# Routing in three groups of tiles and an expert-by-expert result combine, in a Perceiver block with a mixture of experts

## The reference, cut to what matters

```python
xf = layernorm(x).reshape(T, 512)
logits = xf @ gate_w.T                          # 8 experts
probs = softmax(logits)
top_p, top_i = top_k(probs, 2)
w = top_p / (sum(top_p) + 1e-9)
capacity = int(1.25 * T / 8)                    # 160
oh = one_hot(top_i, 8)
rank = cumsum(oh, axis=0) - 1                   # per choice k and expert, over the tokens
keep = sum(rank * oh) < capacity
comb = einsum(w * keep, oh)                     # (T, 8)
for e in range(8):
    y = (silu(xf @ gate_proj_w[e].T) * (xf @ up_proj_w[e].T)) @ down_proj_w[e].T
    out = out + comb[:, e:e+1] * y              # hidden width 1024
x = x + out
```

## Time and profile before

| | us |
|---|---|
| median of 3 runs (range) | 1016.68 (1015.19 to 1021.68) |
| profiled execution, device time | 1016.95 |
| its span in the trace | 1015.2 |
| TensorE busy in the span | 996.6 |
| VectorE busy | 618.2 |
| ScalarE busy | 397.7 |
| GpSimd busy | 210.7 |

### The profile page before, as it was taken

One profiled execution on the slowest core, in us unless ns is written; L12 is line 12 of the kernel. 1 busy time (PEld: TensorE's weight loads), 2 busy tenths in 40 slices (PEclk: granted clock), 3 DMA queues, 4 the chain that ended last, 5 costly groups with the idle time before them and its releaser, 6 DMA issues.

```text
span 1015.2 us, 14027 instructions
## 1 busy us (share of the span) xinstructions
PE 996.6 (98%) x5188; PEld 761.7 (75%) x5188; DVE 618.2 (61%) x1191; ACT 397.7 (39%) x638; POOL 210.7 (21%) x188
## 2 busy tenths in 40 slices
PE   7999999999999999999999999999999999999998
PEld 4886444444454558878888888898999999999997
DVE  6268443445656565896466766677666666656666
ACT  2332211213111143355667542534544544445441
POOL 2053400002000036454422124720000000000051
PEclk9999999999999999999999998999999999999999
DMA  9809589999999922023311100885664656645443
GB/s 290 316 1 389 242 341 422 406 410 396 411 390 408 375 81 82 1 86 112 109 46 34 32 2 6 303 264 174 183 196 139 204 168 184 186 154 181 153 143 135
DMA packets 45511, 206.91 MB, mean 204 GB/s; under 512 B 5536, under 2 KB 16032, under 8 KB 41232
## 3 DMA queue, kind: packets, MB, share of 16 engines
q1 hardware_dynamic: 40256, 187.95, 51.4%
q0 software_dynamic: 5200, 18.22, 5.1%
HBM read 190.04 MB, written 16.12 MB: 203 GB/s over the span
## 4 chain that ended last, share of the span: by engine, by line
PE 87%; DVE 8%; issue 1%; ACT 1%; DMA 1%; SPq 0%; POOL 0%; ACTq 0%; DVEq 0%
PE ps L476 28%; PE ps L892 20%; PE ps L908 10%; PE ps L640 9%; PE ps L611 8%; PE ps L470 1%; PE ps L588 1%; PE ps L621 1%; DVE stats L1278 1%; PE ps L644 1%; PE ps L933 1%; ACT w L1203 1%; PE ps L802 1%; DMA xr<-in_x 1%; PE ps L522 1%
## 5 line engine op out<-in xcount | busy, mean ns | idle before, releaser
L892 PE MATMUL ps<-x,w 128*128 128x320 f32 x1536 | 235.3, 309 | 2.2 <-DVE x L1861 1.1
L892 PEld LDWEIGHTS ps<-x,w 128*128 128x128 f32 x1536 | 230.0, 188 | 7.6 <-DVE w L1802 1.4
L1802 DVE TENSOR_TENSOR w<-big,w 128x1536 fp32r<-128x1536 f32 x64 | 112.4, 1758 | 80.7 <-ACT w L1203 80.1
L908 PE MATMUL ps<-w,hsplit 128*128 128x512 f32 x512 | 128.8, 393 | 0.0
L1203 ACT CAST w<-big 128x1536 fp32r<-128x1536 f32 x64 | 94.4, 1479 | 29.5 <-PE ps L908 29.5
L908 PEld LDWEIGHTS ps<-w,hsplit 128*128 128x128 f32 x512 | 93.3, 188 | 16.5
L611 PE MATMUL ps<-big 128*64 128x512 f32 (+2 forms) x512 | 98.2, 499 | 0.6 <-DVE s_stat L1458 0.6
L476 PE MATMUL ps<-xcT,u 128*128 128x512 f32 x432 | 98.2, 389 | 0.0
L476 PEld LDWEIGHTS ps<-xcT,u 128*128 128x128 f32 x432 | 81.0, 188 | 17.1 <-DVE xcT L1590 0.2
L640 PE MATMUL ps<-big 128*64 128x512 f32 x384 | 89.5, 599 | 2.1 <-DVE big L1437 0.5
L1232 ACT CAST hsplit<-big 128x320 fp32r<-128x320 f32 x64 | 29.4, 460 | 136.1 <-DVE big L1834 134.3
(11 more groups left out here) (337 smaller groups left out, 1528.6 us busy)
## 6 DMA issues: line engine op xcount, KB each, us to landing
big<-in_ctxT SPq DMA_DIRECT2D x16, 3202.0 KB, 16.6
big<-in_ctx SPq DMA_DIRECT2D x16, 3072.0 KB
big<-in_w_units SPq DMA_DIRECT2D x64, 768.0 KB, 4.3
big<-in_dense_units SPq DMA_DIRECT2D x41, 256.0 KB, 2.7
xs<-big POOLq DMA_DIRECT2D x1, 5120.0 KB, 17.4
big<-in_gate_units SPq DMA_DIRECT2D x12, 384.0 KB, 2.9
hr<-xs SPq DMA_DIRECT2D x28, 160.0 KB, 5.5
ys<-big POOLq DMA_DIRECT2D x7, 512.0 KB, 3.3
```

The source lines that it names most:

```text
L892: mm = nc.tensor.matmul(ps[:, 2 * part + f % 2, 0:SLOTS], wsplit[f % RING][w][:, c:c + P], xsplit[j][x][:, d, :], start=(d == 0 and w + x ...
L908: mm = nc.tensor.matmul(ps[:, 4 + s, :], x, w, start=(f == 0 and k == 0), stop=(f == FC - 1 and k == len(terms) - 1))
L1802: V.tensor_tensor(wsplit[f % RING][1][:], wraw[f % RING], wsplit[f % RING][0][:].bitcast(F32), ALU.subtract).then_inc(w_low, 1)
```

## The change

Two parts. Routing goes in three groups of tiles, `ROUTED = ((0, 4), (4, 7), (7, 8))`. For the first two the logits come in two steps: the four chunks of the inner dimension go to four blocks of 32 output rows (`logit_parts`), ScalarE copies that out, and a product with a 0/1 matrix sums the four blocks and turns them back (`logit_sums`). TensorE's order interleaves all this with `wo` and the first expert's rows.

Results are combined expert by expert. `out` gets the x before the experts at once. A DRAM table `tab` of one row of two floats (token number, weight) per slot is scattered with 16 indirect DMAs and read back as `slot_meta`. For each expert GpSimd gathers the rows of `out` that its slots belong to, VectorE adds the weighted results (`mix_held`, in the next expert), and GpSimd scatters them back. Expert 7 takes the same way. The matrix of `pick_last`, its transposes, `last_rows`, `ys`, `gath` and the final stores are gone.

```diff
@@ dense_groups
-    g += [("t5", i) for i in range(4)] + [("lg", 0), ("rk", 0), ("t5", 4), ("lg", 2)]
-    g += [("t5", i) for i in (5, 6, 7)] + [("lg", 1), ("rk", 1)]
-    g += [("gx", d) for d in range(DC)]
+    g += [("t5", i) for i in range(4)] + [("lp", 0), ("lg", 0), ("rk", 0), ("t5", 7)]
+    g += [("t5", i) for i in (4, 5, 6)] + [("lp", 1), ("rk", 1), ("lg", 1), ("lg", 2), ("rk", 2)]
+    g += [("gx", d) for d in (3, 0, 1, 2)]
@@ block.sync
+            sp.dma_start(out[T:T + SLOTS, :], a["x"][0:SLOTS, :]).then_inc(out_begun, 16)
...
+            def output_begun(lo, hi):
+                for i in range(lo, hi):
+                    wait_evacuated(sp, "wo", i)
+                sp.dma_start(out_rows[:, lo:hi, :], xr[:, lo:hi, :]).then_inc(out_begun, 16)
...
-            for i in range(NT):
-                sp.wait_ge(out_ready, i + 1)
-                sp.dma_start(out_rows[:, i, :], xr[:, i, :]).then_inc(out_done, 16)
-            sp.wait_ge(out_done, 16 * NT)
+            sp.wait_ge(mix_out, 16 * NS * NE)
@@ block.tensor
+            def logit_parts(g, n):
+                wait_bank_free(pe, "lp", g)
+                for d in range(DC):
+                    mm = nc.tensor.matmul(bank("lp", g)[d * Q:(d + 1) * Q, 0:n * P], gwT[:].rearrange("p c e -> p (c e)"),
+                                          hT5[:, d, 0:n * P], start=True, stop=True)
+                signals_filled(mm, "lp", g)
+            def logit_sums(g, n):
...
+                for i in range(n):
+                    mm = nc.tensor.matmul(bank("lg", g)[:, i * NE:(i + 1) * NE], lnw[:, 6, tok(i)], swap[:, 0:NE],
+                                          start=True, stop=True)
+                signals_filled(mm, "lg", g)
...
+            transposed_tiles(0, 3)
+            output_chunks(6, 0, 2)
+            transposed_tiles(3, 4)
+            output_chunks(6, 2, 5)
...
+            logit_parts(0, 4)
+            output_chunks(6, 5, 6)
+            output_chunks(7, 0, 1)
+            logit_sums(0, 4)
+            output_chunks(7, 1, 4)
             ranks_within(0)
+            output_chunks(7, 4, 5)
+            ranks_before(1)
+            output_chunks(7, 5, 6)
+            transposed_tiles(4, 7)
+            first_expert_rows(3, 0)
...
+            logit_parts(1, 3)
+            first_expert_rows(0, 0)
+            logit_sums(1, 3)
             transposed_tiles(7, 8)
+            first_expert_rows(1, 0)
             logits(2, 7, 7, 7)
             ranks_within(1)
             first_expert_rows(2, 0)
+            ranks_before(2)
+            first_expert_rows(3, 1)
+            first_expert_rows(0, 1)
+            ranks_within(2)
+            first_expert_rows(1, 1)
+            first_expert_rows(2, 1)
             for d in range(DC):
+                first_expert_rows(d, 2)
@@ block.scalar: logit_parts_out(0, 4) and (1, 3); rows_high(5) to rows_high(7) move behind last_transposed(7)
-            picks_out(NT - 1)
-            act.wait_ge(y_out[1], 32 * (NE // 2 - 1))
-            for s in range(NS):
-                act.wait_ge(last_done, s + 1)
-                nc.scalar.copy(y_last[0][:, s, :], ps[:, 4 + s, :]).then_inc(last_high, 1)
+            tail_out(NE - 1, last=True)
@@ block.vector
             last_apply(4)
+            last_apply(5)
+            last_norm(6)
             choose(0, 0, 4)
+            last_apply(6)
             one_hot(0)
             positions(0)
+            pick_rows(0)
             last_norm(7)
             last_apply(7)
             choose(1, 4, 7)
             one_hot(1)
             positions(1)
             pick_rows(1)
+            choose(2, 7, 8)
+            one_hot(2)
+            positions(2)
+            pick_rows(2)
...
+            def slot_rows():
+                dve.wait_ge(meta_in, 16 * NS)
...
+            def mix_held(n):
+                dve.wait_ge(mix_in, 16 * NS * (n + 1))
+                for s in range(NS):
+                    mix(n, s, held[0:slots_of(s), s, :], held_mixed)
+            def mix_last():
+                dve.wait_ge(mix_in, 16 * NS * NE)
+                for k, s in enumerate(LAST_ORDER):
+                    dve.wait_ge(last_done, k + 1)
+                    if s == NS - 1:
+                        dve.wait_ge(tail_high, NE)
+                        mix(NE - 1, s, ytail[0:LAST, :], mix_step)
+                        dve.wait_ge(mix_step, 1)
+                    mix(NE - 1, s, ps[0:slots_of(s), 4 + s, :], y_evac)
@@ block.vector, expert(), step f, behind the low parts of hid(f)
+                    if f == 3 and n == 1:
+                        slot_rows()
+                    if not first and f == (5 if n == 1 else 3 if last else 4):
+                        mix_held(n - 1)
                     if not (last and f + AHEAD >= FC):
                         split_low(n + (f + AHEAD) // FC, (f + AHEAD) % FC)
-                    if first and 2 <= f < 2 + NT // 2:
-                        pick_last_rows(2 * (f - 2))
-                    if first and f == FC - 2:
-                        pick_last_again()
@@ block.gpsimd, behind the scatter to xs
+            pool.wait_ge(idx_done, len(ROUTED) + 1)
+            pool.wait_ge(down_done, FC)
             for i in range(NT):
                 for k in range(TOPK):
+                    G.indirect_dma_start(tab, bass.IndirectOffsetOnAxis(scat[:, TOPK * i + k:TOPK * i + k + 1], 0),
+                                         token_meta[:, i, k, :], None).then_inc(tab_out, 16)
+            pool.wait_ge(tab_out, 16 * NT * TOPK)
+            slot_tab = tab[0:TRASH, :].rearrange("(n r) w -> r n w", r=SLOTS)
+            for s in range(NS):
+                lo, hi = s * P, min(s * P + P, SLOTS)
+                pool.dma_start(slot_meta[0:hi - lo, :, s, :], slot_tab[lo:hi, :, :]).then_inc(meta_in, 16)
+            pool.wait_ge(out_begun, 16 * 4)
+            pool.wait_ge(rows_set, 2)
...
+            for n in range(NE):
+                if n:
+                    pool.wait_ge(mix_out, 16 * NS * n)
+                for s in range(NS):
+                    m = slots_of(s)
+                    G.indirect_dma_start(mixed_rows[0:m, s, :], None, out, ...).then_inc(mix_in, 16)
+                for k, s in enumerate(LAST_ORDER if n == NE - 1 else range(NS)):
+                    m = slots_of(s)
+                    pool.wait_ge(held_mixed if n < NE - 1 else y_evac, n * NS + k + 1)
+                    G.indirect_dma_start(out, ..., mixed_rows[0:m, s, :], None).then_inc(mix_out, 16)
```

More of the change, by code:

```diff
@@ L33 @@
 LAST = SLOTS - (NS - 1) * P
+ROUTED = ((0, 4), (4, 7), (7, 8))
+LAST_ORDER = (0, 2, 1)
 TRASH = NE * SLOTS
@@ L434, in _ @@
             load(slot_ids, a["slot_ids"], slots_in)
-            for i in range(4, NT):
+            load(swap[:, 0:NE], a["chunk_sum"], slots_in)
+            out_rows = out[0:T, :].rearrange("(i p) d -> p i d", p=P)
+            def output_begun(lo, hi):
+                for i in range(lo, hi):
+                    wait_evacuated(sp, "wo", i)
+                sp.dma_start(out_rows[:, lo:hi, :], xr[:, lo:hi, :]).then_inc(out_begun, 16)
+            output_begun(0, 4)
+            output_begun(4, 6)
+            for i in range(6, NT):
                 wait_filled(sp, "wo", i)
@@ L444, in _, with expert_loads @@
             load_rows(1, 1)
-            def expert_loads(n, j, last=False):
+            def expert_loads(n, j, copies=False, last=False):
                 for f in range(FC):
                     load_unit(n, f)
+                    if copies and f == 1:
+                        output_begun(6, NT)
                     if f == 0 and not last:
@@ L838, in first_expert_rows @@
                     wait_bank_free(pe, "gx", d)
-                for i in range(4 * h, 4 * h + 4):
+                for i in range(*ROUTED[h]):
                     pe.wait_ge(row_low, i + 1)
@@ L900, in down @@
                 h, wh, wl = hsplit[f % 2], wsplit[f % RING][0][:, 2 * DC * P:UW], wsplit[f % RING][1][:, 2 * DC * P:UW]
-                for s in range(NS):
+                for s in LAST_ORDER if final else range(NS):
                     if f == 0 and not first:
@@ L913, in down @@
                     mm.then_inc(down_done, 1)
-            def transpose_picks(i):
-                pe.wait_ge(picked, 3 + NT // 2)
-                if i:
-                    pe.wait_ge(pick_out, i)
-                for s in range(NS):
-                    mm = nc.tensor.transpose(ps[:, 7, s * P:(s + 1) * P], pick_last[:, i, s * P:(s + 1) * P], ident[:])
-                mm.then_inc(pick_done, 1)
-            def last_rows(i, s):
-                b = (0, 1, 2, 3, 7, 0, 1, 2)[i]
-                if s == 0:
-                    pe.wait_ge(pick_out, i + 1 if i < 4 else NT)
-                    if i > 4:
-                        pe.wait_ge(out_ready, i - 4)
-                pe.wait_ge(last_low, s + 1)
-                for part in range(2):
-                    mm = nc.tensor.matmul(ps[:, b, :], pick_lastT[:, s, tok(i)], y_last[part][:, s, :],
```

(23 more changed lines are left out.)

253 lines of the change are left out of this document (106 added, 147 removed).

## The result

The changed kernel takes 1024.74 us (median of 8 runs, 1022.19 to 1027.72), the kernel before in the same group 1016.77 (8 runs): ratio 1.0069, 95% interval 1.0048 to 1.0091. The forecast was 1023.1; the time is within 1% of the kernel before, on the slow side. The profiled execution has a span of 1022.0 us instead of 1015.2, so 6.8 us have to be found.

What follows compares the result with a forecast made beforehand. TensorE, busy 98% of the span, was taken as the bound. Savings of 0.4, 0.5, 2.6 and 6.9 (-10.4) against +16.6 in expert 1 gave +6.2 on 1016.95: 1023.1 us, range 1006 to 1033.

Steps and rivals of the forecast that it cites:

- The end: From the last `down`'s start to program end: combining by scatters takes 10.0 us instead of 16.9, saving 6.9.
- routing: Routing up to expert 0's start: VectorE's chain level with TensorE, 0.4 us gained, between a loss of 2 and +3.
- expert 1: Step 3 of expert 1: VectorE waits for `slot_meta`, TensorE stands 13.8 us; with late `mix_held(0)` and lower clock +16.6.
- expert 0: Expert 0: the 1.04 us wait at 695.80 goes, later `xs` scatters cost some 0.5; net 0.5 us gained.
- Rival 1: Scatters to `tab`: 8-byte rows far cheaper than 2 KB ones, table hidden, TensorE doesn't stop; 1006.5 us, chance 15%.
- The last expert: Expert 7 without transposes: seven steps take 5.35 us instead of 5.70, the eighth saves 0.2; 2.6 us saved.
- the end is D + 10.0: D is the start of the last `down`; additions, three scatters and landing end 10.0 us later, instead of 16.9.
- Rival 4: Routing gives nothing or costs 2 us, the rest as forecast: 1025.5 us; chance counted in the forecast's 55%.
- the forecast's case: Whole kernel: the main forecast of 1023.1 us, its own range 1015 to 1029, chance 55%.
- The steady experts: Experts in steady state: `mix_held` adds 2.25 us of VectorE to one step; costed at nothing, at most 4 us.
- rival 3: All experts: `mix_held` makes VectorE late, 4 us, on a mild stop of 6, clock not lost; 1016.5 us, 10%.
- Rival 2: Slot table: small pieces slow, `slot_meta` at 743, 22 us of standstill in expert 1; 1031.6 us, chance 20%.

Runs made afterwards that it cites:

- table_early: Changed kernel without GpSimd's wait for expert 0's last `down` before the 16 scatters to `tab`; 1009.74 us, ratio 0.9926.
- ask_late: Changed kernel with `slot_rows` in step 6 of expert 1 instead of 3 and `mix_held(0)` in step 7 instead of 5; 1020.26 us, ratio 1.0023.
- the version with the moved splits: Changed kernel without GpSimd's wait before the `tab` scatters, and both `split_low` moved out of the chain before expert 0; 1007.76 us, ratio 0.9886.
- routing_only: The kernel before with the change of the routing alone; 1018.91 us, ratio 1.001.
- the two that were made from it for the drain: Moved `split_low` and early `tab` scatters, plus behind GpSimd's last scatter a wait for the landing (1009.54 us) or a memset (1008.29 us).

## Why the forecast came out right

The sum was right to 1.6 us (to 0.7 against the profiled execution, 1023.78), and this closeness is in part luck. The end was priced 3.4 us too good and routing 1.1, expert 1 some 2.5 us too dear and expert 0 some 0.8, and the work ahead of all that happened to be 0.6 us shorter: together 0.6 us. The mechanism that decides, the stop in expert 1, was right; that of the end was not.

**Expert 1, +14.1 instead of +16.6: right in mechanism.** It was put together from GpSimd's start at 700.6 (700.99), 22.5 us for the 16 (22.96), landing 3.5 (4.48), three plain DMAs 2.0 (2.59), and their landing 6. Only this last one was far off: from the end of the third issue at 731.02 to VectorE's start at 732.76 are 1.7 us, and the view of the DMA issues from 722 to 740 us puts two of these loads at 3.1 us from issue to landing and the third at 2.4. The 2560 pieces of 8 bytes aren't dear here. So `slot_meta` was there at 732.8 instead of 734.6. Queued behind it were 4.4 us of VectorE (4.6), the `down` would have started at 724.99 (725.4) and started at 737.18, 12.2 us late. `mix_held(0)` caused no wait of its own. The clock behind the stop stood at 0.50 and cost 744.44 - 737.18 - 5.35 = 1.9 us (2.3).

Rival 1, that small rows make the scatters cheap, is answered by one comparison within this trace. While VectorE stood still, from 716.68 on, the scatters came every 1.26 us without exception, 0.96 of issue and 0.30 between, for 1 KB each; that is the floor of those of 256 KB as well. The price is in the issue, not in the bytes. The first ten, beside VectorE at work, took 15.69 us, 1.57 each. With VectorE at work throughout, the early table's 16 took 26.35 us and the late one's 26.1.

Why beside VectorE at work it is more, the forecast read wrongly. The scatter at 712.60 met this operation of VectorE:

```profile
712.53 1.76 DVE L1830 TENSOR_TENSOR w<-big,w 128x1536 fp32r<-128x1536 f32 x1 [1.51 <-ACT w L1225]
```

1.69 us of it were left, and the scatter took 2.52. Over the scatters to `tab` that began inside an operation with two inputs in SBUF, the traces of the changed kernel and of the early table give one rule:

| left of VectorE's operation, us | 1.69 | 1.64 | 1.54 | 1.29 | 1.01 | 0.53 | 0.35 |
|---|---|---|---|---|---|---|---|
| the scatter took, us | 2.52 | 2.48 | 2.37 | 2.12 | 1.85 | 1.36 | 1.18 |

That is what was left, less 0.13, and then 0.96: a full stop, in every such row. Beside operations that read PSUM or have one input they paid nothing (0.96 with 0.55 us left of a COPY out of PSUM; in the version with the moved splits 0.96 inside the four `first_expert_low`). The Trainium skill (SBUF — State Buffer, on the shared port pair) has GpSimd fully blocked while VectorE runs a two-port operation, or one with two inputs in SBUF where GpSimd's own reads SBUF. `split_low` is a `tensor_tensor`, and of these the same section of the Trainium skill says that they have no two-port mode and that a probe didn't see them stall a DMA; here they stall indirect DMAs, and the measurement decides. The forecast took `split_low` for a two-port operation, and said that the trace agrees in direction only, since 2.54 is less than 2.7 and most others paid far less. But at 653.35 the operation had 1.70 us left, which gives 2.53, and those that paid less began late in one or beside none. 22.5 us came out because VectorE stood still for six of the 16; with it at work the traces give 26.1 and 26.4. `ask_late` missed in part because I carried the number of a standing VectorE over to a working one, and in part by the longer landing.

**The last expert, -2.6: right.** Its steps take 5.35 us (1001.40 - 996.04 = 5.36), as in every other expert.

**The end, -3.5 instead of -6.9: the step that failed is "the end is D + 10.0".** D is 1008.59. VectorE's last addition was done at 1012.93, D + 4.34 (4.35 forecast), the third scatter issued at D + 6.1 (5.96), and the data had landed by D + 7.9, 2 us sooner than I said (1.8 us behind the issue, nearer to the forecast's good bound of 2.1 than to its 4.1). But I had taken the landing for the end of the program. The end is the latest of all engines' ends, and GpSimd's, 8.8 us of drain that began at D + 4.4, came at D + 13.2. Nothing in the chain of waits of the kernel before pointed at it; its row was in the trace, under the program's closing line, and I hadn't read it. With it the end would have been D + 13.4 and the forecast 3.4 us higher.

**Routing, +0.73 in the profile instead of -0.4: the chain was right, three numbers were not.** VectorE did bound it: TensorE had its expert rows done at 648.3 and waited 3.82 us. (The 649.0 that the forecast's timetable gives for this doesn't follow from the terms it shows: 652.2 + 1.3 - 2.3 is 651.2. Nothing in the sum hung on it.) By the common mark `gate_up` starts 36.6 us behind the first transposes, 37.4 before: 0.8 gained. What was wrong: first, `logit_parts` cost half of my 2.1 us.

```profile
620.88 1.06 PE L822 MATMUL ps<-big,gwT 128*32 128x512 f32 x8
621.87 0.73 PE L487 MATMUL ps<-wou,gh 128*128 128x512 f32 x2
```

Eight records of 512 columns in 1.0 us: the four blocks of 32 rows run at once, a little over the low bound of 0.85 to 3.4. The Trainium skill says so (TensorE: Matmul & The Clock Gate, why this matters for your kernels): small outputs in different column groups run concurrently; the trace agrees, and I had left that rule out. Since VectorE was the bound, it made no difference to the end. Second, `positions(1)` took 2.6 us instead of 1.2. Two of its operations took 0.54 and 1.20 us, where they take 0.17 in `positions(0)`, and each ended 0.03 us behind a subtraction of GpSimd; the second pair:

```profile
640.26 1.20 DVE L1735 SCALAR_TENSOR_TENSOR rt<-rt 128x6 f32<-128x6 f32 x1
...
640.16 1.27 POOL L1987 TENSOR_TENSOR row7low<-hr,row7high 128x512 fp32r<-128x512 f32 x1
```

So VectorE seems to be held up by GpSimd as well, in the chain that bounds routing; no run moves these subtractions. Third, the wait of 3.82 us was priced as a wait alone. I said that the clock should stay up, and at 621 it did, where it was 0.50 before; but behind the wait it stood at 0.50, and the first 48 matmuls took 8.80 us instead of 7.27, 1.5 us that turned the gain of 0.8 into a loss. In the other kernels with the same wait the first `down` comes 46.5 us behind the mark instead of 45.2 (46.56, 46.49 and 46.53 in `routing_only`, `table_early` and `ask_late`), a loss of 2 us against the 44.5 of the kernel before. The times don't show it: `routing_only` has 1018.91 against 1016.54, but 0.7 of that lies outside the span (2.4 us of its device time, 1.7 in the kernel before), and the ratio's interval holds 1. Nor is 44.5 the old routing's number. Its five profiles give 44.5, 44.5, 49.5, 49.9 and 50.9 us, the last three with the second stretch at the lower clock shown above; no profile of the new routing has one that long. By these profiles the new routing loses up to 2 us against an execution in which the old one has only its first stretch, and gains some 3 to 5 against the others. Rival 4, that routing gives nothing or costs 2 us, is what happened, within the forecast's case. The version with the moved splits has 41.9, since neither the long wait nor the lower clock is left; the two that were made from it for the drain have 43.5 and 44.0, their clock having fallen once earlier in the routing.

**Expert 0, -1.27 instead of -0.5.** The wait of 1.04 us in front of expert 1 is gone, as forecast. The loss set against it didn't come: the scatters to `xs` began at 641.60, not 643.7, and SyncE began to load rows at 669.51, earlier than before.

**The steady experts, 0: right.** `mix_held` takes 2.06 us, VectorE has it to spare, and no other wait of TensorE is in the list. That closes rival 3. Rival 2's price for small pieces, 743 for the table, is 10 us too high.

## What to carry to other kernels

Give the preparation of a new stage its own time before the engines need it, and ask of each wait that holds it back what it protects; and when the consumer is moved, reckon with its second wait and with a producer that gets slower beside a busy engine. A wait on TensorE can cost itself and the lower clock behind it (here one of 3.8 us in front of expert 0 did in four profiles of four, one of 1.1 to 2.8 us in none of eight), so the last microseconds of a chain in front of it are worth more than they look. For the end of a program read the last rows of every engine's queue, not only the landing of the last data.

## What the runs showed of the hardware

- GpSimd's queue drains 4.0 us behind a last memset or plain store, 4.5 behind an indirect gather and 7.0 to 7.2 behind indirect scatters, whether these have landed or not. In the changed kernel it sets the end, 5.3 us behind the last data (1021.8 against 1016.5).
- An indirect DMA of 128 rows costs GpSimd 1.26 us at the least, for 8-byte rows as for rows of 2 KB, and 1.57 to 1.69 on average beside this VectorE at work. One that begins inside a VectorE operation with two inputs in SBUF takes what is left of it less 0.13 us, and then its 0.96 (0.35 to 1.69 us left, 1.18 to 2.52 taken).
- The landing of a row of 16 such scatters took 4.48, 6.16 and 7.60 us in three kernels; it was the shortest where VectorE and TensorE stood still.
- Where the clock falls in the routing changes from execution to execution and from kernel to kernel: at 620 in the kernel before, at 629, 642 or 652 in others, for 3 to 7 us each time, and in three of the five profiles of the old routing once more, from 638 on for 10 to 14 us.
- The scatter between runs of one kernel goes with the mean granted clock. In the 30 runs of the kernel before beside the first experiments it was 0.998 in the nine of 1014.6 to 1015.7 us, 0.993 in the six of 1019.1 to 1020.7, and 0.988 to 0.990 in the four of 1022.5 to 1023.7.
